# A first pass of attention that takes one head and all keys at a time

## The chip, the cores and the metric

The kernel runs on one core of a Trainium2 chip. The metric is the device time of one execution, in microseconds (us), as the median of the runs shown.

## The reference

One block of a gated cross-attention model, with batch 4, 1024 tokens, width 512, a context of width 1024, and 8 heads of 64. Cut to what matters:

```python
src_trans = einsum('bsf,of->bso', src, W_src) + b_src        # keys and values, from the context
tgt_trans = einsum('btf,of->bto', layernorm(x), W_tgt) + b_tgt   # queries
src_trans, tgt_trans = both times the mask
scores = einsum('bthd,bshd->bhts', q, k) / sqrt(64)
scores = where(src_mask == 0, -inf, scores)
attn = softmax(scores, axis=-1)
tgt_update = einsum('bhts,bshd->bthd', attn, v)
x = x + tanh(g_xattn) * (concat([layernorm(x), tgt_update]) @ W_out.T + b_out)
x = x + tanh(g_ffn) * ffn(layernorm(x))     # int8-like activations, ternary weights, depthwise conv of 3, silu
```

## The kernel before

The program has four stages, one after the other: queries and the part of the output that doesn't need attention (A), keys and values (B), attention (C), and the feed-forward part (D). Only stage C is changed. Each engine has its own hand-written program; semaphores order them.

**Two passes over the scores.** A pair of heads has its 64-row operands in partitions 0 to 63 (head 0) and 64 to 127 (head 1), so that two matmuls, one of each head, use separate halves of TensorE's rows. There are 16 pairs (4 batches x 4 pairs), numbered g. The *first pass* (`tops`, PE line 1244) computes rough scores, queries down the partitions, keys along the columns, only to find each query's maximum. VectorE (line 926) reads them from PSUM, adds the mask's row and keeps the minimum of the negated values. The *second pass* (`score`, line 1260) computes the scores exactly, keys down the partitions, 512 queries along the columns, in four terms (high x high, low x high, high x low, and the row maxima by a small matmul), and ScalarE exponentiates 1024 columns (both heads) at once (line 684). `product` (line 1272) multiplies the exponentials by the values, and each of its two matmuls appears as two passes in the trace.

**Units and macros.** Both passes are cut into 256 units, 16 per pair of heads. A unit of the first pass is 128 queries, both heads and 512 of the 1024 keys: two matmuls. A unit of the second pass is 128 keys, both heads and 512 queries: eight matmuls. TensorE's loop runs 134 *macros* s. A macro holds the second pass of units 2s and 2s+1, the products of units 2s-2 and 2s-1, and the first pass of units 2s+22 and 2s+23; the first pass is `LEAD` = 22 units ahead, and its first 22 units are a lead-in of their own before macro 0. From macro 117 on no first pass is left.

**PSUM banks.** Of the eight banks of 512 columns, the first pass uses bank 4 (head 0) and bank 5 (head 1), the second pass 0 and 1 (even units) and 2 and 3 (odd units), the products 6 and 7. Bank 4 also takes the transpose of the row maxima (`rows`, line 1279) and the row sums (`sums`, line 1285). Bank 5 also takes the output projection (`project`, twelve matmuls in `split_mm`, lines 1224 to 1226). VectorE counts what it has read from the two banks in the semaphores `dve_free4` and `dve_free5`. A first pass waits on the one and the other.

**What stands at a macro's end.** After the products of some macros come: `rows` in macros 8g-3; `sums` in macros 4k+6 for block k of 8 units; `project` in the 24 macros 32 to 39, 64 to 71 and 96 to 103, and eight more in the last macros. VectorE then casts the transposed maxima twice (lines 944 and 946), or transposes the sums (`zt`, line 950), or adds the projection to `bx` (line 975, `finish`). In the macro behind a `sums`, VectorE inverts the sums and normalises (`inverse`, `normal`); two macros behind it ScalarE copies the high part (`upper`, line 692) between its two exponentials and VectorE subtracts it (`lower`, line 968) between its reads for the two units of the first pass. GpSimd adds up the exponentials (line 667).

In macros with a projection the two banks of the first pass are taken in reverse order. VectorE collects 32 minima in `nmv` and folds the two key halves in one small reduction per pair of heads (line 933).

## Time and profile before

| what | value |
|---|---|
| runs before | 1923.99, 1928.58 and 1927.51 us; median 1927.51 |
| the profiled execution | 1929.86 us, of which the span of the trace is 1928.0 us |
| busy in the span | TensorE 1684.4 us (87%), VectorE 1216.9 (63%), ScalarE 780.3 (40%), GpSimd 729.0 (38%) |
| chain that ended last | TensorE 62%, issue 19%, GpSimd 7%, VectorE 6%, DMA 5% |
| its first lines | second pass (L1260) 13%, products (L1272) 12%, keys and values (L1224 to L1226) 9% each, first pass (L1244) 6% |
| VectorE's reads of the first pass (L926) | 512 of 689 ns, 333.4 us busy |

A row of a timeline gives the start in the span, the length, the engine, the line and the operation with output and inputs, how many instructions were merged, and in brackets the idle time before and what ended it. A matmul's length includes its way through the array, so that neighbours overlap; the distance between two starts is what one costs. PEld is the load of a matmul's weights. `64*128` and `128*64` are the part of the array that a matmul uses.

### The profile page before, as it was taken

The page shows a single profiled execution, that of the slowest core. Times are in us where ns is not written, and L with a number is a line of the kernel's source. Part 1 is how long each engine was busy: PE and PEld are TensorE (multiplying, and loading weights), DVE is VectorE, ACT ScalarE, POOL GpSimd, SP SyncE. Part 2 cuts the span into 40 slices and gives each one's busy share as a digit, 9 for nine tenths or more (in the row PEclk, how much of TensorE's full clock was granted, in tenths as well). Part 3 has the DMA queues.
Part 4 walks back from the last instruction along what each step waited for, and adds up shares of the span by engine and source line. Part 5 has one row for each costly group of instructions (what it writes and reads, how often), then busy time and mean ns, then how long its engine had stood idle before and what let it go on. Part 6 is the DMA issues. An engine that isn't in the chain of part 4 may idle for free.

```text
span 1928.0 us, 24398 instructions
## 1 busy us (share of the span) xinstructions
PE 1684.4 (87%) x8738; PEld 1038.8 (54%) x8738; DVE 1216.9 (63%) x2270; ACT 780.3 (40%) x793; POOL 729.0 (38%) x317
## 2 busy tenths in 40 slices
PE   6887899999997699999999999999856785967867
PEld 5666678888885344455445444544433443534434
DVE  6777645343433567755765676465269979799793
ACT  2111122222210044433442344245318766787676
POOL 1121000000000088866885688578606134062340
PEclk9989999999998599999999999999979798997988
DMA  6656547444444511114111412041130030120201
GB/s 233 229 181 206 179 170 243 154 149 152 171 145 152 180 56 56 56 66 143 56 57 66 143 57 100 12 143 35 44 131 1 1 131 0 38 92 0 88 1 44
DMA packets 104676, 200.59 MB, mean 104 GB/s; under 512 B 7568, under 2 KB 27024, under 8 KB 104592
## 3 DMA queue, kind: packets, MB, share of 16 engines
q1 hardware_dynamic: 104592, 199.49, 29.5%
q8 instruction: 50, 0.82, 0.2%
q14 instruction: 34, 0.28, 0.0%
HBM read 127.90 MB, written 71.57 MB: 103 GB/s over the span
## 4 chain that ended last, share of the span: by engine, by line
PE 62%; issue 19%; POOL 7%; DVE 6%; DMA 5%; SPq 1%; ACT 1%; POOLq 0%; DVEq 0%; ACTq 0%
PE ps L1260 13%; PE ps L1272 12%; PE ps L1224 9%; PE ps L1226 9%; PE ps L1225 9%; PE ps L1244 6%; DMA wraw<-in_w2T 5%; POOL h_first L672 4%; POOL h_third L672 2%; PE ps L1285 2%; DVE junk L926 1%; PE ps L1461 1%; DVE h_first L1179 1%; POOL acc L667 1%; DVE gp L1158 1%
## 5 line engine op out<-in xcount | busy, mean ns | idle before, releaser
L667 POOL TENSOR_TENSOR acc<-acc,pr 128x1024 f32<-128x1024 f32 x192 | 457.7, 2384 | 118.7 <-ACT pr L684 99.6
L684 ACT ACTIVATE pr<-ps,mcol 128x1024 f32<-128x1024 f32 x256 | 284.3, 1114 | 405.1 <-PE ps L1260 402.3
L926 DVE CUSTOM_DVE_ANT_0 junk<-ps,mbias 128x512 bf16<-128x512 f32 x512 | 333.4, 689 | 171.8 <-PE ps L1244 168.0
L1272 PE MATMUL ps<-pr,vv 128*64 128x512 f32 x1024 | 273.3, 616 | 0.0
L672 POOL TENSOR_TENSOR h_first<-h_first,last_tap 128x1024 f32<-128x1024 f32 x44 | 104.8, 2385 | 306.2 <-ACT last_tap L804 306.2
L650 POOL MEMSET nmt<- 128x128 f32 x1 | 0.2, 204 | 449.1 <-DMA w_ternary<-wtb 449.1
L1244 PE MATMUL ps<-kh,qh 64*128 64x512 f32 x512 | 136.8, 475 | 26.3 <-DVE nmv L926 17.6
L1244 PEld LDWEIGHTS ps<-kh,qh 64*128 64x128 f32 x512 | 57.5, 193 | 148.3 <-issue 101.7
L1419 PE MATMUL ps<-xiT,w1q 128*128 128x512 bf16 x512 | 125.1, 393 | 5.9 <-ACT xiT L790 5.9
L1461 PE MATMUL ps<-w2q,hq 128*128 128x512 bf16 x512 | 120.8, 390 | 2.5 <-ACT hq L840 1.8
L667 POOL TENSOR_TENSOR acc<-pr 128x1024 f32<-128x1024 f32 x32 | 76.8, 2399 | 110.8 <-ACT pr L684 110.8
L1260 PE MATMUL ps<-qh,kh 64*128 64x512 f32 x512 | 116.2, 445 | 0.0
L1448 PE MATMUL ps<-ident,h_first 128*128 128x128 f32 x352 | 57.8, 317 | 66.2 <-DVE h_first L1179 51.8
L1260 PE MATMUL ps<-qh,kl 64*128 64x512 f32 x512 | 102.5, 392 | 0.0
L1260 PE MATMUL ps<-maug,aug 64*128 64x512 f32 x512 | 102.3, 391 | 0.0
L1260 PE MATMUL ps<-ql,kh 64*128 64x512 f32 x512 | 102.0, 390 | 0.0
L1224 PE MATMUL ps<-chh,wsh 128*128 128x512 f32 x256 | 99.7, 389 | 1.7 <-DVE chl L1091 1.7
L1224 PE MATMUL ps<-wsh,chh 128*128 128x512 f32 x256 | 99.7, 389 | 0.3 <-DVE cst L1133 0.3
L1226 PE MATMUL ps<-wsh,chl 128*128 128x512 f32 x256 | 99.6, 389 | 0.0
L1225 PE MATMUL ps<-wsl,chh 128*128 128x512 f32 x256 | 99.6, 389 | 0.0
L1225 PE MATMUL ps<-chl,wsh 128*128 128x512 f32 x256 | 99.6, 389 | 0.0
L1226 PE MATMUL ps<-chh,wsl 128*128 128x512 f32 x256 | 99.6, 389 | 0.0
(152 smaller groups left out, 3179.7 us busy)
## 6 DMA issues: line engine op xcount, KB each, us to landing
craw<-in_ctxT SPq DMA_DIRECT2D x8, 2048.0 KB, 9.7
xa<-in_x SPq DMA_DIRECT2D x8, 1024.0 KB, 6.4
wraw<-in_w1T SPq DMA_DIRECT2D x16, 512.0 KB, 7.3
wraw<-in_w2T SPq DMA_DIRECT2D x16, 512.0 KB, 7.6
q_split<-kqh SPq DMA_DIRECT2D x32, 256.0 KB, 2.0
q_split<-kql SPq DMA_DIRECT2D x32, 256.0 KB, 2.3
base<-lna SPq DMA_DIRECT2D x8, 1024.0 KB, 9.1
k_split<-kqh SPq DMA_DIRECT2D x32, 256.0 KB, 2.2
```

The lines of the kernel that those rows point to most:

```text
L667: nc.gpsimd.tensor_tensor(acc[:, blk % 2, :], first, pr[:, (8 * blk + j) % NP, :], ALU.add).then_inc(pool_acc, 1)
L672: nc.gpsimd.tensor_tensor(h[j % 3], h[j % 3], last_tap[j % 2][:], ALU.add).then_inc(pool_tap, 1)
L684: act.activation(pr[:, u % NP, :], ps[:, 2 * (u % 2):2 * (u % 2) + 2, :].rearrange("p a t -> p (a t)"), ACT.Exp, bias=mcol[:, (u // 64) * ...
L926: dve.tensor_tensor_reduce(out=junk[:, e, :], in0=ps[:, 4 + e, :], in1=mbias[:, b % 2, kk * CH:(kk + 1) * CH], scale=-1.0, scalar=3.0e38, ...
L1224: pe.matmul(acc, lh, rh, start=k == 0, stop=False)
L1225: pe.matmul(acc, lh, rl, start=False, stop=False)
L1226: last = pe.matmul(acc, ll, rh, start=False, stop=k == n - 1)
L1244: last = pe.matmul(ps[:, 4 + e, :], qh[g % 3][64 * e:64 * e + 64, i * P:(i + 1) * P], kh[g % 3][64 * e:64 * e + 64, kk * CH:(kk + 1) * CH] ...
L1260: last = pe.matmul(ps[:, 2 * (u % 2) + e, :], of_keys[64 * e:64 * e + 64, :], of_tokens[64 * e:64 * e + 64, :], start=w == 0, stop=w == 3)
L1272: last = pe.matmul(ps[64 * e:64 * e + 64, 6 + blk % 2, :], vv[:, g % 2, j, 64 * e:64 * e + 64], pr[:, u % NP, e * CH:(e + 1) * CH], start= ...
L1419: last = pe.matmul(ps[:, 2 * (j % 2) + t, :], w1q[:, k, j * P:(j + 1) * P], xiT[:, k, t * 512:(t + 1) * 512], start=k == 0, stop=k == KD - 1)
L1461: last = pe.matmul(ps[:, i % 2, :], hq[:, i % 2, j, :], w2q[:, j, :], start=j == 0, stop=j == KH - 1)
```

## The change

The first pass is cut the other way: a unit is now 128 queries, *one* head and all 1024 keys, so that its two matmuls are the two key halves of one head, in banks 4 and 5. Even units are head 0, odd units head 1. One VectorE operation reads both banks, 1024 columns, and writes the minimum straight into `nmt`, which gets two halves used in turn; `nmv`, the fold and `dve_nm` go. Both banks now have one semaphore, `dve_free`, and a planner (`take`) notes for each use of the banks which use it has to wait for. In the lead-in odd units use banks 0 and 1.

TensorE's loop is written as two streams. In each of ten slots there is one matmul of head 0 and one of head 1. Head 0 has the even unit's first pass in slots 0 and 1 and its scores in slots 2 to 9; head 1 has its scores in slots 0 to 7 and the odd unit's first pass in slots 8 and 9. Then come the products of both units, with nothing between them, and `rows`, `sums` and `project` as before. The semaphore for ScalarE is now raised by head 0's last score, in slots 5 and 9.

```diff
+        def take(use, banks):
+            after[use] = max(held.get(bank, 0) for bank in banks)
+            done[use] = len(done) + 1
+            for bank in banks:
+                held[bank] = done[use]
+
+        def first_bank(n):
+            return 4 if n >= LEAD or n % 2 == 0 else 0
+
         for n in range(LEAD):
-            use4["a", n], use5["b", n] = len(use4), len(use5)
+            take(("m", n), (first_bank(n), first_bank(n) + 1))
...
         def c_dve(dve):
             def tops(n):
-                g, i, kk = n // 16, n % 16 // 2, n % 2
-                b = g // PAIRS
+                g, i, e = n // 16, n % 16 // 2, n % 2
+                b, bank = g // PAIRS, first_bank(n)
                 if n % 64 == 0 and b:
                     bias(b)
-                if n % 16 == 0 and g:
-                    dve.wait_ge(dve_nm, g)
-                for e, free, use in heads(n):
-                    dve.wait_ge(pe_mx, n + 1)
-                    c = (8 * e + i) * 2 + kk
-                    dve.tensor_tensor_reduce(out=junk[:, e, :], in0=ps[:, 4 + e, :], in1=mbias[:, b % 2, kk * CH:(kk + 1) * CH], scale=-1.0,
-                                             scalar=3.0e38, op0=ALU.add, op1=ALU.min, accum_out=nmv[:, c:c + 1]).then_inc(free, 1)
-                if n % 16 == 15:
-                    dve.wait_ge(dve_free4, use4["a", n] + 1)
-                    dve.wait_ge(dve_free5, use5["b", n] + 1)
-                    if g:
-                        dve.wait_ge(pe_mt, g)
-                    dve.tensor_reduce(nmt[:, 0:16], nmv[:].rearrange("p (c k) -> p c k", k=2), AX.X, ALU.min).then_inc(dve_nm, 1)
+                if n % 16 == 0 and g >= 2:
+                    dve.wait_ge(pe_mt, g - 1)
+                dve.wait_ge(pe_mx, n + 1)
+                if n:
+                    dve.wait_ge(dve_free, done["m", n - 1])
+                dve.tensor_tensor_reduce(out=junk[:], in0=ps[:, bank:bank + 2, :].rearrange("p a t -> p (a t)"), in1=mbias[:, b % 2, :], scale=-1.0,
+                                         scalar=3.0e38, op0=ALU.add, op1=ALU.min, accum_out=nmt[:, g % 2, 8 * e + i:8 * e + i + 1]).then_inc(dve_free, 1)
...
         def c_pe(pe):
-            def tops(n):
-                g, i, kk = n // 16, n % 16 // 2, n % 2
-                if n % 16 == 0:
+            def first(n, half):
+                g, i, e = n // 16, n % 16 // 2, n % 2
+                if n % 16 == 0 and half == 0:
                     pe.wait_ge(sp_qk[g % 3], 32 * (g // 3 + 1))
-                for e, free, use in heads(n):
-                    if use:
-                        pe.wait_ge(free, use)
-                    last = pe.matmul(ps[:, 4 + e, :], qh[g % 3][64 * e:64 * e + 64, i * P:(i + 1) * P],
-                                     kh[g % 3][64 * e:64 * e + 64, kk * CH:(kk + 1) * CH], start=True, stop=True)
-                last.then_inc(pe_mx, 1)
-
-            def score(u):
+                if half == 0 and after["m", n]:
+                    pe.wait_ge(dve_free, after["m", n])
+                scores = pe.matmul(ps[:, first_bank(n) + half, :], qh[g % 3][64 * e:64 * e + 64, i * P:(i + 1) * P],
+                                   kh[g % 3][64 * e:64 * e + 64, half * CH:(half + 1) * CH], start=True, stop=True)
+                if half:
+                    scores.then_inc(pe_mx, 1)
+
+            def score(u, w, e):
...
-                if u >= 2:
+                if w == 0 and u >= 2:
                     pe.wait_ge(act_p, u - 1)
+                if w == 0 and u < 2:
+                    pe.wait_ge(dve_free, done["m", LEAD - 1])
...
+                term = pe.matmul(ps[:, 2 * (u % 2) + e, :], of_keys, of_tokens, start=w == 0, stop=w == 3)
+                if w == 3 and e == 0:
+                    term.then_inc(pe_st, 1)
...
             for s in range(MACROS):
-                for a in range(2):
-                    if 2 * s + a < UNITS:
-                        score(2 * s + a)
-                    if a == 0 and 2 * s + LEAD < UNITS:
-                        tops(2 * s + LEAD)
-                for a in range(2):
-                    if 0 <= 2 * s - 2 + a < UNITS:
-                        product(2 * s - 2 + a)
-                    if a == 0 and 2 * s + LEAD + 1 < UNITS:
-                        tops(2 * s + LEAD + 1)
+                for slot in range(10):
+                    u, n = 2 * s + (slot - 2) // 4, 2 * s + LEAD
+                    if slot < 2 and n < UNITS:
+                        first(n, slot)
+                    if slot >= 2 and u < UNITS:
+                        score(u, (slot - 2) % 4, 0)
+                    u, n = 2 * s + slot // 4, 2 * s + LEAD + 1
+                    if slot < 8 and u < UNITS:
+                        score(u, slot % 4, 1)
+                    if slot >= 8 and n < UNITS:
+                        first(n, slot - 8)
+                for u in (2 * s - 2, 2 * s - 1):
+                    if 0 <= u < UNITS:
+                        product(u)
```

Two places where the order differs. On TensorE, the end of macro 10, which has the row sums, and the beginning of macro 11. Before (L1244 is the first pass, L1272 a product, L1285 the sums, L1260 the second pass):

```order
L1244 MATMUL ps<-kh_108,qh_107 128x512 [waits dve_free4]
L1244 MATMUL ps<-kh_108,qh_107 128x512 [waits dve_free5]
L1272 MATMUL ps<-pr,vv 64x512 [waits act_p]
L1272 MATMUL ps<-pr,vv 64x512
L1285 MATMUL ps<-acc,ones 64x512 [waits dve_free4,pool_acc]
L1285 MATMUL ps<-acc,ones 64x512
L1260 MATMUL ps<-qh_111,kh_112 128x512 [waits act_p]
L1260 MATMUL ps<-qh_111,kh_112 128x512
L1260 MATMUL ps<-qh_111,kl 128x512 x2
L1260 MATMUL ps<-ql,kh_112 128x512 x2
L1260 MATMUL ps<-maug,aug_101 128x512 x2
L1244 MATMUL ps<-kh_108,qh_107 128x512 [waits dve_free4]
```

And now (L1239 is the first pass, L1268 a product, L1280 the sums, L1256 the second pass):

```order
L1239 MATMUL ps<-kh_107,qh_106 128x512 [waits dve_free]
L1256 MATMUL ps<-maug,aug_101 128x512
L1239 MATMUL ps<-kh_107,qh_106 128x512
L1268 MATMUL ps<-pr,vv 64x512 [waits act_p]
L1268 MATMUL ps<-pr,vv 64x512
L1268 MATMUL ps<-pr,vv 64x512 [waits act_p]
L1268 MATMUL ps<-pr,vv 64x512
L1280 MATMUL ps<-acc,ones 64x512 [waits dve_free,pool_acc]
L1280 MATMUL ps<-acc,ones 64x512
L1239 MATMUL ps<-kh_107,qh_106 128x512 [waits dve_free]
L1256 MATMUL ps<-qh_110,kh_111 128x512 [waits act_p]
```

The first pass has moved out from between the products, in front of them and to the head of the next macro, directly behind the sums. On VectorE, macro 12, two macros behind those sums. Before (L926 reads a bank, the second L926 row of each is its accumulator, L963 normalises, L968 is the low part):

```order
L963 TENSOR_TENSOR un<-ps,rb 128x512 [waits pe_pv,dve_inv]
L926 ISA junk,nmv<-ps,mbias 128x512 [waits pe_mx]
L926 ISA nmv 128x1
L926 ISA junk,nmv<-ps,mbias 128x512 [waits pe_mx]
L926 ISA nmv 128x1
L968 TENSOR_TENSOR ul<-un,uh 128x512 [waits act_uh]
L926 ISA junk,nmv<-ps,mbias 128x512 [waits pe_mx]
```

And now (L928 reads both banks, L959 normalises, L964 is the low part):

```order
L959 TENSOR_TENSOR un<-ps,rb 128x512 [waits pe_pv,dve_inv]
L928 ISA junk,nmt<-ps,mbias 128x1024 [waits dve_free,pe_mx]
L928 ISA nmt 128x1
L964 TENSOR_TENSOR ul<-un,uh 128x512 [waits act_uh]
L928 ISA junk,nmt<-ps,mbias 128x1024 [waits dve_free,pe_mx]
```

The low part keeps its place between the two units' reads, and each unit has one read in place of two.

## Rows read from the trace of the kernel before

**Rows 1.** The windows by stage: lead-in, attention, feed-forward; engines' busy us, granted clock, DMA.
```profile
core 0: us, PE busy (x) PEld busy (x) DVE busy (x) ACT busy (x) POOL busy (x), PEclk, DMA share, GB/s
618.77:668.24 49.47, 29.40 (x45) 11.95 (x46) 29.09 (x89) 0.00 (x0) 0.00 (x0) 0.50 0.62 218
678.51:1376.05 697.54, 693.12 (x3921) 334.84 (x3919) 427.27 (x1149) 292.86 (x283) 524.22 (x221) 1.00 0.21 73
1412.00:1928.00 516.00, 367.35 (x2193) 210.90 (x2192) 426.65 (x503) 356.56 (x295) 155.75 (x64) 0.88 0.14 49
```

**Rows 2.** The timeline of TensorE, macro 42: start, length, line, operation, count.
```profile
902.80 0.50 PE L1260 MATMUL ps<-qh,kh 64*128 64x512 f32 x2
903.14 0.40 PE L1260 MATMUL ps<-qh,kl 64*128 64x512 f32 x2
...
903.83 0.39 PE L1244 MATMUL ps<-kh,qh 64*128 64x512 f32 x2
...
905.06 1.08 PE L1272 MATMUL ps<-pr,vv 128*64 128x512 f32 x4
906.07 0.49 PE L1244 MATMUL ps<-kh,qh 64*128 64x512 f32 x2
906.50 1.08 PE L1272 MATMUL ps<-pr,vv 128*64 128x512 f32 x4
907.46 1.08 PE L1285 MATMUL ps<-acc,ones 128*64 128x512 f32 x4
```

**Rows 3.** The timeline of TensorE in macro 120, where no first pass is left.
```profile
1339.42 1.94 PE L1272 MATMUL ps<-pr,vv 128*64 128x512 f32 x8
1341.29 0.50 PE L1260 MATMUL ps<-qh,kh 64*128 64x512 f32 x2
```

**Rows 4.** The timeline of VectorE in macros 42 and 44.
```profile
904.27 0.69 DVE L926 CUSTOM_DVE_ANT_0 junk<-ps,mbias 128x512 bf16<-128x512 f32 x1 [1.06 <-PE ps L1244]
...
904.88 0.69 DVE L926 CUSTOM_DVE_ANT_0 junk<-ps,mbias 128x512 bf16<-128x512 f32 x1
...
908.57 0.72 DVE L950 STREAM_TRANSPOSE zt<-ps 128x512 f32<-128x512 f32 x1 [0.65 <-PE ps L1285]
...
916.10 0.69 DVE L968 TENSOR_TENSOR ul<-un,uh 128x512 fp32r<-128x512 f32 x1
```

**Rows 5.** The timeline of the lead-in: VectorE's first read, later its reads and TensorE's weight load.
```profile
621.24 0.69 DVE L926 CUSTOM_DVE_ANT_0 junk<-ps,mbias 128x512 bf16<-128x512 f32 x1
...
630.63 0.69 DVE L926 CUSTOM_DVE_ANT_0 junk<-ps,mbias 128x512 bf16<-128x512 f32 x1
...
631.38 0.28 PEld L1244 LDWEIGHTS ps<-kh,qh 64*128 64x128 f32 x1 [0.33 <-DVE nmv L926]
632.21 0.69 DVE L926 CUSTOM_DVE_ANT_0 junk<-ps,mbias 128x512 bf16<-128x512 f32 x1 [0.88 <-PE ps L1244]
```

**Rows 6.** The timeline of TensorE and VectorE at macros with a projection.
```profile
848.69 1.08 PE L1285 MATMUL ps<-acc,ones 128*64 128x512 f32 x4 [0.49 <-DVE nmv L926]
...
1378.68 0.39 PE L1226 MATMUL ps<-wo2h,ul 128*128 128x512 f32 x1
...
1379.17 0.75 DVE L975 SCALAR_TENSOR_TENSOR bx<-ps,cst,bx 128x512 f32<-128x512 f32 x1 [4.14 <-PE ps L1226]
...
1380.07 0.47 PE L1224 MATMUL ps<-wo2h,uh 128*128 128x512 f32 x1 [1.01 <-DVE bx L975]
```

**Rows 7.** The timeline of ScalarE in macro 44.
```profile
914.44 1.12 ACT L684 ACTIVATE pr<-ps,mcol 128x1024 f32<-128x1024 f32 x1 [2.46 <-PE ps L1260]
915.45 0.62 ACT L692 ACTIVATE uh<-un 128x512 fp32r<-128x512 f32 x1
```

**Rows 8.** The timeline of TensorE and VectorE at a transpose of the row maxima.
```profile
777.49 0.33 PE L1279 MATMUL ps<-ident,nmt 128*128 128x128 f32 x1
777.75 0.50 PE L1260 MATMUL ps<-qh,kh 64*128 64x512 f32 x2
...
778.17 0.28 DVE L946 TENSOR_TENSOR mt<-ps,mt 16x128 fp32r<-16x128 f32 x1
```

More of the change, by code:

```diff
@@ L334, in flamingo_gated_block @@
         MACROS = 134
-        use4, use5, inv = {}, {}, {}
+        done, after, held, inv = {}, {}, {}, {}
+        def take(use, banks):
[5 more added lines that the diff above has]
+            return 4 if n >= LEAD or n % 2 == 0 else 0
         for n in range(LEAD):
-            use4["a", n], use5["b", n] = len(use4), len(use5)
+            take(("m", n), (first_bank(n), first_bank(n) + 1))
             if n == 15:
-                use4["t", 0] = len(use4)
+                take(("t", 0), (4,))
                 inv["row", 0] = 1
@@ L343, in flamingo_gated_block @@
                 if n < UNITS:
-                    use4["a", n], use5["b", n] = len(use4), len(use5)
+                    take(("m", n), (4, 5))
             if s - 1 in ZBLK:
@@ L1258, in score @@
-                for w, (of_keys, of_tokens) in enumerate(terms):
-                    for e in range(2):
-                        last = pe.matmul(ps[:, 2 * (u % 2) + e, :], of_keys[64 * e:64 * e + 64, :], of_tokens[64 * e:64 * e + 64, :],
-                                         start=w == 0, stop=w == 3)
-                last.then_inc(pe_st, 1)
+                if w == 0 and u < 2:
+                    pe.wait_ge(dve_free, done["m", LEAD - 1])
+                keys, tokens, rows = slice(j * P, (j + 1) * P), slice(t * CH, (t + 1) * CH), slice(64 * e, 64 * e + 64)
@@ L1276, in rows @@
             def rows(g):
-                pe.wait_ge(dve_nm, g + 1)
-                pe.wait_ge(dve_free4, use4["t", g])
-                pe.transpose(ps[:, 4, 0:P], nmt[:], ident[:]).then_inc(pe_mt, 1)
+                pe.wait_ge(dve_free, max(after["t", g], done["m", 16 * g + 15]))
+                pe.transpose(ps[:, 4, 0:P], nmt[:, g % 2, :], ident[:]).then_inc(pe_mt, 1)
             def sums(blk):
                 pe.wait_ge(pool_acc, 7 * (blk + 1))
-                pe.wait_ge(dve_free4, use4["z", blk])
+                pe.wait_ge(dve_free, after["z", blk])
                 for e in range(2):
@@ L1296, in c_pe @@
             pe.wait_ge(pool_zero, 4)
[L1297 to L1312 removed]
+            for n in range(LEAD):
+                first(n, 0)
+                first(n, 1)
+                if n == 15:
+                    rows(0)
+            for s in range(MACROS):
+                for slot in range(10):
[12 more added lines that the diff above has]
+                        product(u)
                 if s in TURNS:
```

47 lines of the change are left out of this document (17 added, 30 removed).

## The prediction

> **What bounds the kernel now.** I read the windows by stage first [rows 1]. The attention stage runs from 678.51 to 1376.05 us. TensorE is busy for 693.1 of those 697.5 us at a granted clock of 1.00, while VectorE has 427 us, ScalarE 293 and GpSimd 524. TensorE is the bound there and everything is priced as its time. In the lead-in ahead (618.77 to 668.24) it is the other way: TensorE and VectorE hand one pair of PSUM banks to and fro, and the clock is at 0.50. The feed-forward stage after 1412 isn't touched and is taken as it is.
>
> The timeline of one macro [rows 2] gives the prices. I write times from its first matmul, and call two matmuls side by side, one of each head, a slot. The first slot takes 0.34 (902.80 to 903.14), each further one 0.23 (three to 903.83), and the turn from the last slot to a product 0.31 (four slots after 903.83 end at 904.75; the product starts at 905.06). A product followed by anything in the other shape takes 1.01 (905.06 to 906.07), and a first pass between two products takes 0.43. So a plain macro is 906.50 + 1.01 - 902.80 = 4.71 us. At the end of the stage, where no first pass is left, two adjacent products take 1339.42 to 1341.29 = 1.87 us [rows 3], so 0.86 + 1.01.
>
> **The plain macro.** Now there are ten slots and then two products. Slot 9 would start at 0.34 + 8 x 0.23 = 2.18, the products at 2.49, and the next macro at 4.36: a gain of 0.35. But the first pass in slots 8 and 9 writes the banks that slots 0 and 1 filled, and waits until VectorE has read both. VectorE starts 0.44 after the slot that it needs (903.83 to 904.27 [rows 4]), so at 0.34 + 0.44 = 0.78. The trace of before has no read of 1024 columns. Two reads of 512 follow each other at 0.61 of which 0.08 is the accumulator's, so 512 more columns add 0.53, and 0.69 + 0.53 = 1.22 (bounds: 1.38 as two whole reads, 1.06 as columns alone). It ends at 2.00. TensorE's next weight load follows a VectorE read by 0.06 in the lead-in (630.63 + 0.69 = 631.32, load at 631.38 [rows 5]). So slot 8 begins at 2.06 in place of 1.95, and as its weights come late it takes 0.34: slot 9 at 2.40, products at 2.71 and 3.57, next macro at **4.58**. The change is -0.13 in each of the 117 macros that still carry a first pass: **-15.2 us**. (Without the slot-8 wait it would be -0.35; with a read of 1.38 about +0.03.) The second read has its data at 2.84, ends at 4.06, and so is done before 4.58.
>
> **The waits at slot 0.** Before, the first pass stood behind four slots of scores. Now it stands at the very front of a macro, and on TensorE's queue all ten slots are behind it. Whatever VectorE last does with banks 4 and 5 is therefore waited for in the open. Four cases:
>
> - *Row sums, every fourth macro.* The sum's matmuls start at 4.43, VectorE's transpose starts 1.11 later and takes 0.72 (907.46, 908.57 [rows 2, 4]). A restart after another shape follows by 0.15 (1379.17 + 0.75 to 1380.07 [rows 6]); I take 0.11 between this and 0.06. The next macro starts at 6.38, which is 1.80 more than a plain one, where it is 0.95 more today (907.46 + 1.01 - 902.80 = 5.67). That is +0.85. Of 28 such macros with a first pass behind, 22 have no projection that hides the transpose: **+18.7**.
> - *Two macros later.* VectorE's low part of the normalised rows stands between the two reads and waits for ScalarE's copy, which stands behind the exponential of the even unit. That unit now ends its scores in slot 5 (1.26) and not in slot 3. Exponential at 1.26 + 0.44 = 1.70, with VectorE's distance from a slot to its reader, copy 1.01 later and 0.62 long (914.44, 915.45 [rows 7]), so until 3.33; low part 3.37 to 4.06 (0.69, [rows 4]). The second read then runs 4.06 to 5.28, and the next macro starts at 5.39 in place of 4.58: +0.82 in 27 macros, **+22.1**. Today the same chain fits: the low part begins at 916.10 and nobody waits for it.
> - *Row maxima to rows.* The small transpose starts at 4.58, VectorE's two casts end 0.96 later (777.49 to 778.17 + 0.28) and the restart is 0.11; unstalled the step takes 0.26 (777.49 to 777.75 [rows 8]). +0.80 in the 11 macros where no projection follows: **+8.8**.
> - *Projection, 24 macros.* From the last of its twelve matmuls to the restart of TensorE behind VectorE's update takes 1378.68 to 1380.07 = 1.39 [rows 6], measured where the kernel already has this wait; the plain turn is 0.31. +1.08 each: **+25.9**. Against this, nine macros with a projection today stand still for 0.49 and restart late because the banks are read in turn (848.69 [rows 6]); now the read is over by 4.06, ahead of the sum at 4.43. About -0.6 each: **-5.4**.
>
> **Ends of the stage.** In macros 117 to 127 there is no first pass but the heads stay two slots apart, so ten slots hold eight slots' work: 11 x 2 x 0.23 = **+5.1**. In the lead-in two pairs of banks now alternate. Today a unit takes (668.24 - 621.24) / 22 = 2.14 us, of which VectorE reads 1.30 (0.61 + 0.69); it starts reading at 621.24 [rows 1, 5]. Behind a released bank pair the matmuls need 0.06, 0.83 to the first half's data (631.38 to 632.21) and 0.46 for the second half (a slot at half the clock), 1.35 in all, and then the read itself 1.22, for every two units. So a unit costs about 1.28: 2.5 to the first read + 22 x 1.28 + 2.5 for the row transpose, which nothing overlaps, = 33.2. **-16.3** (-13 if the second half's weights aren't loaded ahead). The small VectorE reduction per pair of heads, which folded the minima of the two key halves, goes, and so do half of the reads; both lie beside TensorE's work and are taken at nothing beyond what stands above; ScalarE and GpSimd have room (GpSimd 524 of 697 us, and the macros get longer).
>
> **Sum.** -15.2 + 18.7 + 22.1 + 8.8 + 25.9 - 5.4 + 5.1 - 16.3 = +43.7 us on the profiled run's 1929.9 us, so 1973.6. The median of the runs is 2.4 us lower: **1971 us**, 2.3% slower.
>
> **A rule on the weight loads.** In the lead-in the second head's weight load waits until its own bank has been read (631.38), and no later load passes it. The Trainium skill (TensorE: Matmul & The Clock Gate, Step-by-step: what each phase is for) says that TensorE may pull a weight load ahead of running matmuls when the row groups don't conflict, and keeps the matmuls in order. By that rule the restart's extra 0.11 would be hidden at each of some 84 waits, -9 us; the late slot in the row speaks against it.
>
> **Rivals.**
> *Faster: the waits are not in the open.* If a held first pass held only its own head, and the other head's matmuls ran on past it, the four slot-0 terms and the slot-8 wait would go: -41 - 5.4 + 5.1 - 16.3 = -58, so 1870 us. The waits are 75.5 + 117 x 0.22 = 101 us in all; this case decides once more than 44 of them, 43%, are hidden. For it: the two heads use separate rows of the array and separate banks. Against it: 848.69 and 1380.07 show the whole engine idle behind one waiting matmul. 7%.
> *Near no change:* the same, for about half of the waits. 6%.
> *Slower still: the clock.* In the lead-in TensorE is busy 29.4 of 49.5 us and is granted 0.50 [rows 1]. The new waits of 0.8 to 1.1 us come in 78 or so macros. If one in five of these let the clock fall for a macro, which would then cost about 4 us more (ten slots and two products at half the clock, 4.36 more at the most), that is +60: 2030 us. Against it: the stage as it is stays at 1.00 through the idles of 0.49 at 848.69; idles of 0.8 to 1.1 no row of it shows. The Trainium skill (TensorE: Matmul & The Clock Gate, A second HAM failure mode: psum-queue depth-cycling) tells of a kernel whose short idles between groups of matmuls, while PSUM banks are cycled, made the clock swing; this is the case that speaks against the change. 7%.
> *The heads don't run side by side* when their matmuls belong to different steps: ten slots at 0.43 or so, +2.0 x 117 = +234: 2205 us. Today's pairs already differ in weights, data and bank. 3%.
> The forecast keeps 77%.
>
> **Chances.** A measurement tells about 0.3% (6 us) from no change. Faster 0.08 (the first rival and a stray of the second), same 0.05, slower 0.87. For the range: no slot-8 wait takes 26 us off, 1945; a read of 1.30 with restarts of 0.15 everywhere adds some 20 us, 1992. I take 1943 to 1995, which leaves out the rivals on either side.
>
> **What the profile after would show.** Plain macros of 4.58 us (4.36 if slot 8 doesn't wait); products as groups of eight passes at 1.87; VectorE reads of 1.22; TensorE idle 0.8 to 1.1 us ahead of the first pass behind each sum, projection and row transpose and two macros after each sum; the lead-in some 33 us long. Wrong would be: macros behind a sum as short as plain ones, a granted clock under 1.00 in the stage, or slots of more than 0.23.

## The result, and the profile after

The changed kernel takes **1961.62 us** (median of 4 runs, 1960.06 to 1961.83) where the kernel before took 1926.83 in the same comparison (4 runs, 1923.99 to 1928.58): a ratio of 1.018, 95% interval 1.0163 to 1.0198, so 1.8% slower. The forecast was 1971 us, in a range of 1943 to 1995. The profiled execution took 1961.83 us, with a span of 1960.0.

The windows by stage of the changed kernel, with the columns of [rows 1]: the lead-in, attention from macro 2 to the last sum ahead of the final projections, and the rest.

```profile
core 0: us, PE busy (x) PEld busy (x) DVE busy (x) ACT busy (x) POOL busy (x), PEclk, DMA share, GB/s
614.56:649.88 35.32, 25.64 (x46) 10.51 (x47) 28.52 (x48) 0.00 (x0) 0.00 (x0) 0.50 0.83 290
659.69:1406.43 746.74, 679.84 (x3921) 365.23 (x3919) 404.63 (x672) 283.43 (x283) 524.08 (x221) 1.00 0.19 68
1406.43:1960.00 553.57, 394.30 (x2294) 229.82 (x2292) 436.78 (x516) 358.44 (x297) 161.62 (x67) 0.89 0.14 49
```

TensorE has *less* to do in the attention stage than before (679.8 us in place of 693.1, since products now stand together), but it stands idle for 67 us of it, where it stood idle for 4. The five waits listed below add up to those 67 us. The granted clock stayed at 1.00. The page puts 54% of the chain that ended last on TensorE (62% before) and 8% on VectorE (6%). Who was waited for, in the list of waits from 660 to 1420 us (columns: who waited, for whom, us in total, times, longest):

```profile
PE ps L1239 <- DVE bx L971: 20.8, 24, 0.9
PE ps L1239 <- DVE zt L946: 18.0, 22, 0.8
PE ps L1239 <- DVE nmt L928: 16.4, 24, 1.0
PE ps L1239 <- DVE mt L942: 7.5, 11, 0.7
PE ps L1220 <- DVE nmt L928: 4.1, 6, 0.7
```

These are the four slot-0 waits of the prediction: 24 behind projections, 22 behind sums, 11 behind row transposes, and those for a read. Of the 24 for a read, 21 are macros two behind a sum (0.59 to 0.69 us each), and three are at slot 8, where VectorE prepared the mask's row first (1.03 to 1.04 us); six more macros two behind a sum have a projection, which waits for the read instead (L1220). Now the timeline of TensorE around one of each (L1239 is the first pass, L1256 the second, L1268 the products, L1280 the sums):

```profile
900.10 0.50 PE L1239 MATMUL ps<-kh,qh 64*128 64x512 f32 x1
...
902.07 0.39 PE L1256 MATMUL ps<-ql,kh 64*128 64x512 f32 x1
902.16 0.49 PE L1239 MATMUL ps<-kh,qh 64*128 64x512 f32 x1
...
902.49 0.39 PE L1239 MATMUL ps<-kh,qh 64*128 64x512 f32 x1
902.82 1.94 PE L1268 MATMUL ps<-pr,vv 128*64 128x512 f32 x8
904.59 1.03 PE L1280 MATMUL ps<-acc,ones 128*64 128x512 f32 x4
906.43 0.49 PE L1239 MATMUL ps<-kh,qh 64*128 64x512 f32 x1 [0.82 <-DVE zt L946]
...
909.14 1.94 PE L1268 MATMUL ps<-pr,vv 128*64 128x512 f32 x8
911.01 0.50 PE L1239 MATMUL ps<-kh,qh 64*128 64x512 f32 x1
...
913.73 1.94 PE L1268 MATMUL ps<-pr,vv 128*64 128x512 f32 x8
916.36 0.46 PE L1239 MATMUL ps<-kh,qh 64*128 64x512 f32 x1 [0.69 <-DVE nmt L928]
```

The macro from 900.10 carries the sums: 6.33 us (5.67 in [rows 2]). The one from 906.43 is a plain macro: 911.01 - 906.43 = 4.58, and the next one, two behind the sums, takes 5.35. The products stand together (909.14 to 911.01 = 1.87, as in [rows 3]), and head 1's first pass at 902.16 is 0.09 late against head 0's slot beside it (902.07). VectorE in the same stretch:

```profile
900.87 1.22 DVE L928 CUSTOM_DVE_ANT_0 junk<-ps,mbias 128x1024 bf16<-128x1024 f32 x1 [1.30 <-PE ps L1239]
...
905.66 0.72 DVE L946 STREAM_TRANSPOSE zt<-ps 128x512 f32<-128x512 f32 x1 [1.50 <-PE ps L1280]
...
914.38 0.69 DVE L964 TENSOR_TENSOR ul<-un,uh 128x512 fp32r<-128x512 f32 x1 [1.36 <-ACT uh L694]
914.99 1.22 DVE L928 CUSTOM_DVE_ANT_0 junk<-ps,mbias 128x1024 bf16<-128x1024 f32 x1
```

The read of 1024 columns takes the 1.22 us of the forecast; 256 of them have a mean of 1222 ns. It begins 0.44 behind the slot that it needs (900.43 to 900.87) and ends at 902.09, and the first pass that wants its banks starts at 902.16. The low part has waited for ScalarE's copy until 914.38 and keeps the second read back until 914.99, so that the read ends at 916.21 and TensorE starts again at 916.36.

### The profile page after: what moved, and what is told of

It is laid out like the page before. It is cut to its first block, busy times and chain, and to the rows that moved or that the text cites. A ratio compares the mean times of both kernels' runs of the same rounds, so it can differ in the third digit from the quotient of the medians.

```text
span 1960.0 us, 24095 instructions
## 1 busy us (share of the span) xinstructions
PE 1664.0 (85%) x8738; PEld 1065.9 (54%) x8738; DVE 1194.5 (61%) x1742; ACT 770.7 (39%) x793; POOL 728.3 (37%) x317
## 4 chain that ended last, share of the span: by engine, by line
PE 54%; issue 21%; POOL 9%; DVE 8%; DMA 5%; ACT 1%; SPq 1%; POOLq 0%; ACTq 0%; DVEq 0%
PE ps L1256 9%; PE ps L1220 9%; PE ps L1268 9%; PE ps L1222 9%; PE ps L1221 9%; PE ps L1239 6%; POOL h_first L674 5%; DMA wraw<-in_w2T 4%; DVE junk L928 3%; POOL h_third L674 3%; PE ps L1460 2%; POOL acc L669 1%; PE ps L1280 1%; DVE bx L971 1%; ACT uh L694 1%
## 5 line engine op out<-in xcount | busy, mean ns | idle before, releaser
L928 DVE CUSTOM_DVE_ANT_0 junk<-ps,mbias 128x1024 bf16<-128x1024 f32 x256 | 313.0, 1222 | 155.5 <-PE ps L1239 152.5
L1239 PE MATMUL ps<-kh,qh 64*128 64x512 f32 x512 | 195.5, 467 | 79.6 <-DVE nmt L928 24.5
L1268 PE MATMUL ps<-pr,vv 128*64 128x512 f32 x1024 | 247.7, 605 | 0.0
L1256 PE MATMUL ps<-qh,kh 64*128 64x512 f32 x512 | 205.1, 420 | 0.7 <-DVE nmt L928 0.7
L1256 PE MATMUL ps<-maug,aug 64*128 64x512 f32 x512 | 191.9, 391 | 0.0
L1256 PE MATMUL ps<-qh,kl 64*128 64x512 f32 x512 | 191.6, 391 | 0.0
L1256 PE MATMUL ps<-ql,kh 64*128 64x512 f32 x512 | 191.1, 390 | 0.0
L1239 PEld LDWEIGHTS ps<-kh,qh 64*128 64x128 f32 x512 | 79.3, 195 | 192.7 <-DVE nmt L928 78.9
L1268 PEld LDWEIGHTS ps<-pr,vv 128*64 128x64 f32 x1024 | 62.2, 136 | 120.0 <-issue 119.7
L1220 PE MATMUL ps<-chh,wsh 128*128 128x512 f32 x256 | 99.7, 389 | 1.7 <-DVE chl L1087 1.7
L1256 PEld LDWEIGHTS ps<-qh,kh 64*128 64x128 f32 x512 | 90.7, 185 | 19.0 <-issue 6.0
L1220 PE MATMUL ps<-wsh,chh 128*128 128x512 f32 x256 | 99.7, 389 | 0.3 <-DVE cst L1129 0.3
```

The costliest lines, as they stand in the source:

```text
L928: dve.tensor_tensor_reduce(out=junk[:], in0=ps[:, bank:bank + 2, :].rearrange("p a t -> p (a t)"), in1=mbias[:, b % 2, :], scale=-1.0, sca ...
L1220: pe.matmul(acc, lh, rh, start=k == 0, stop=False)
L1239: scores = pe.matmul(ps[:, first_bank(n) + half, :], qh[g % 3][64 * e:64 * e + 64, i * P:(i + 1) * P], kh[g % 3][64 * e:64 * e + 64, half ...
L1256: term = pe.matmul(ps[:, 2 * (u % 2) + e, :], of_keys, of_tokens, start=w == 0, stop=w == 3)
L1268: last = pe.matmul(ps[64 * e:64 * e + 64, 6 + blk % 2, :], vv[:, g % 2, j, 64 * e:64 * e + 64], pr[:, u % NP, e * CH:(e + 1) * CH], start= ...
```

## The experiments

Each kernel is the changed kernel with one edit, unless it says otherwise. The comparisons had the kernel before at 1926.16 (e1 to e4), 1925.48 (e5, e7 to e9) and 1926.61 us (e6, e10).

My theory: the time is the occupancy of banks 4 and 5. A unit holds both of them from its first matmul to the end of the read, 0.34 + 0.44 + 1.22, and 0.06 until TensorE is back: 2.06 us, twice in a macro that wants to take 4.36. Nothing fits between, so each further user of these banks (sums, row maxima, projection) and each delay of a read (the low part) lengthens the macro. The rivals: the adjacent products or the two streams are themselves slow; the merged read is what costs; the waits are only partly in the open.

**e1_lower: the low part behind the second read.**

```diff
-                    if a == 0 and s - 2 in ZBLK:
+                    if a == 1 and s - 2 in ZBLK:
                         lower(ZBLK[s - 2])
```

> The changed kernel with one move: VectorE's low part of the normalised rows (lower) stands behind the second read of the macro, not between the two reads. If the forecast's second term is right (the low part waits for ScalarE's copy and holds up the second read, and that the next macro's first slot), the macros two behind a row sum fall from 5.24 to 5.34 us to the plain 4.58: 27 x 0.70 = -19 us, 1942 us. If something else set those macros (ScalarE's own delay, or a wait that only moves to another place), less than 5 us.

Measured: 1949.96 us (ratio to the kernel before 1.013, interval 1.0113 to 1.0147). That is 11.7 us less than the changed kernel and 8 us more than expected. The 28 macros two behind a sum fell by 18.4 us, close to the 19 expected (22 without a projection from 115.7 to 100.9 us, six with one from 55.5 to 51.9). But 6.9 us came back (the expectation of e6 puts it at up to 7.7): three macros in which the first unit of a new batch needs the mask's row took 7.74, 9.40 and 8.99 us in place of 6.86, and one with sums behind them 7.69 in place of 6.34. The timeline at the first of them, VectorE and GpSimd:

```profile
755.82 2.51 POOL L669 TENSOR_TENSOR acc<-pr 128x1024 f32<-128x1024 f32 x1 [1.17 <-ACT pr L686]
756.00 2.88 DVE L933 TENSOR_SCALAR mbias<-mbias 128x1024 f32<-128x1024 f32 x1
```

The operation that turns the mask into a bias takes 0.69 us at the stage's start. Here it began while GpSimd added, and took 2.88: until 758.88, 0.55 behind the end of the addition (758.33). In the changed kernel itself it began later in the addition, and took 2.23, again until 0.55 behind its end (757.85 + 2.38 = 760.23, and 760.78):

```profile
757.85 2.38 POOL L669 TENSOR_TENSOR acc<-pr 128x1024 f32<-128x1024 f32 x1 [1.19 <-ACT pr L686]
758.55 2.23 DVE L933 TENSOR_SCALAR mbias<-mbias 128x1024 f32<-128x1024 f32 x1
...
762.10 0.49 PE L1239 MATMUL ps<-kh,qh 64*128 64x512 f32 x1 [1.04 <-DVE nmt L928]
```

In every kernel here in which VectorE does it beside an addition of GpSimd, it ends 0.55 or 0.56 us behind that addition, whether it took 1.22, 1.9 or 2.9 us. So the mask operation doesn't run slowly beside GpSimd; it stands still until GpSimd is done. The Trainium skill (SBUF — State Buffer, SBUF: two separate sides) says so: the port pair that VectorE and GpSimd share is locked for a whole instruction by whichever came first, and the other is fully blocked, where VectorE's operation is of a kind that wants that pair. The trace agrees.

**e2_banks: sums and row maxima in bank 2, projection in bank 3.** These banks hold the odd unit's scores, and are free once ScalarE has exponentiated them; the odd unit's scores come only in the middle of the next macro.

```diff
+                if w == 0 and after.get(("s", u, e)):
+                    pe.wait_ge(dve_free, after["s", u, e])
...
-                pe.transpose(ps[:, 4, 0:P], nmt[:, g % 2, :], ident[:]).then_inc(pe_mt, 1)
+                if g:
+                    pe.wait_ge(act_p, 16 * g - 4)
+                pe.transpose(ps[:, 2 if g else 4, 0:P], nmt[:, g % 2, :], ident[:]).then_inc(pe_mt, 1)
...
+                pe.wait_ge(act_p, min(8 * blk + 14, UNITS))
...
-                    last = pe.matmul(ps[64 * e:64 * e + 64, 4, :], ones...
+                    last = pe.matmul(ps[64 * e:64 * e + 64, 2, :], ones...
...
+                pe.wait_ge(act_p, min(64 * (b + 1) + 2 * i + 2, UNITS))
-                split_mm(pe, ps[:, 5, :],...
+                split_mm(pe, ps[:, 3, :],...
```

> The changed kernel with the row sums and the transposed maxima in bank 2 and the projection in bank 3 (an odd unit's score banks, which TensorE needs again only from slot 4 on), so that the first pass in slot 0 waits for nothing but the last read. If the slot-0 waits are what makes the change slower: sums 6.33 to 5.44 (22 times), transposed maxima 5.66 to 4.85 (11), projection 8.44 to 7.52 (24): -19.6 - 8.9 - 22.1 = -51 us, 1911 us, and the two-behind macros stay at 5.3. If these macros are long because of VectorE's work itself, the time moves by less than 10 us.

Measured: 1907.39 us (0.9902, 0.9885 to 0.9918), so the changed kernel with other banks for these three is 1% *faster* than the kernel before. TensorE's timeline at a sum (L1242 is the first pass, L1288 the sums):

```profile
905.38 1.94 PE L1273 MATMUL ps<-pr,vv 128*64 128x512 f32 x8
907.15 1.03 PE L1288 MATMUL ps<-acc,ones 128*64 128x512 f32 x4
908.11 0.49 PE L1242 MATMUL ps<-kh,qh 64*128 64x512 f32 x1
```

The first pass follows the sums by 0.96 with no idle time. Macros with sums take 5.44 in place of 6.33, with row maxima 4.91 for 5.66, with a projection 7.53 for 8.44; those two behind a sum stay at 5.25, which this edit shouldn't touch, and plain ones at 4.58.

**e3_two_reads: the unit's two halves read and released one by one.**

```diff
-                dve.tensor_tensor_reduce(out=junk[:], in0=ps[:, bank:bank + 2, :]..., accum_out=nmt[...]).then_inc(dve_free, 1)
+                for half in range(2):
+                    dve.tensor_tensor_reduce(out=junk[:, half * CH:(half + 1) * CH], in0=ps[:, bank + half, :],
+                                             ..., accum_out=nmv[:, c:c + 1]).then_inc(dve_free, 1)
+                if n % 16 == 15:
+                    dve.tensor_reduce(nmt[:, g % 2, 0:16], nmv[:].rearrange("p (c k) -> p c k", k=2), AX.X, ALU.min).then_inc(dve_free, 1)
...
-                if half == 0 and after["m", n]:
-                    pe.wait_ge(dve_free, after["m", n])
+                if after["m" if half else "h", n]:
+                    pe.wait_ge(dve_free, after["m" if half else "h", n])
```

> The changed kernel, but each unit is read by two operations of 512 columns again, each with its own bank's release (and the small fold per pair of heads is back). If the merged read costs by holding both banks until its end, slot 8 no longer waits: plain macros 4.58 to 4.36, -26 us, and some 5 us more where slot 0 needs only one of the banks: 1930 us. If the number of VectorE instructions mattered, it would be slower than the changed kernel by up to 256 x 0.08 = 20 us.

Measured: 1931.05 us (1.0022, 1.001 to 1.0034), the total expected, though not by the terms expected. Two reads of 512 back to back take VectorE 1.23 us until its next operation starts (916.99 to 918.22 in its timeline), where the one read takes 1.14 (757.41 to 758.55 in that of the changed kernel), but the first bank is given back after 0.69 of them. The plain macros directly behind a sum took 4.38 us in place of 4.58. But 11 others, directly behind a macro that is two behind a sum, took 4.72 to 4.76: the low part still delays the second read, and slot 1 now waits for its second half (926.17, 0.61 behind slot 0 in place of 0.34). The rest came mainly where slot 0 now waits for bank 4 alone: macros two behind a sum take 4.80 us (5.26), and the 24 with a projection 201.8 in all (213.2). Those with sums take 6.12 (6.33).

**e4_products: the kernel *before*, with its odd first pass ahead of the two products.** This brings the products together without streams or a merged read.

```diff
+                if 2 * s + LEAD + 1 < UNITS:
+                    tops(2 * s + LEAD + 1)
                 for a in range(2):
                     if 0 <= 2 * s - 2 + a < UNITS:
                         product(2 * s - 2 + a)
-                    if a == 0 and 2 * s + LEAD + 1 < UNITS:
-                        tops(2 * s + LEAD + 1)
```

> The kernel before with one move: the odd unit's first pass stands ahead of the two products, which are then adjacent; units, reads and banks as before. If keeping the products together were enough, plain macros would go from 4.71 to 4.36, -41 us: 1886 us. If the banks' release rules (first pass at slot 4, second bank read until 2.83, and the next first pass wants it at 2.18), plain macros take about 5.1 us, +49 us: 1976 us.

Measured: 1968.53 us (1.0214, 1.0197 to 1.0231). TensorE:

```profile
949.48 0.50 PE L1260 MATMUL ps<-qh,kh 64*128 64x512 f32 x2
...
951.71 1.10 PE L1244 MATMUL ps<-kh,qh 64*128 64x512 f32 x2
952.74 1.94 PE L1272 MATMUL ps<-pr,vv 128*64 128x512 f32 x8
954.61 0.50 PE L1260 MATMUL ps<-qh,kh 64*128 64x512 f32 x2
```

A plain macro is 954.61 - 949.48 = 5.13. The two units of the first pass (950.52 and 951.71) are now so close together that the second waits for the reads of the first, one bank after the other, and the products are held behind it: 1.03 us from 951.71 to 952.74 in place of 0.31. The same mechanism, without any of the change's other parts. Products side by side are worth having only if the first pass doesn't pay for it.

**e5_one_lead: banks 4 and 5 alone in the lead-in** (`first_bank` returns 4).

> The changed kernel with the lead-in's odd units in banks 4 and 5 too, so that one pair of banks is handed to and fro. If the lead-in's gain (49.5 us to 35.3) comes from the second pair of banks, a unit takes 0.06 + 0.83 + 0.46 + 1.22 = 2.57 us, the lead-in about 61 us: +26 us on the changed kernel's 1961.6, 1988 us, longer than even the lead-in of the kernel before, because one long read holds both banks. If it comes from the fewer and longer VectorE reads, it stays within 5 us of 1962.

Measured: 1985.32 us (1.0314, 1.0295 to 1.0333). From the first first pass to macro 2 it took 684.46 - 615.88 = 68.6 us in place of 45.1, and the macros were the same. The second pair of banks is worth 23.5 us to a lead-in of one-head units.

**e6_banks_lower, e7_all, e10_masks: the cures together.** e6 is e2 and e1, with the read of 1024 columns kept; e7 adds the two reads of e3; e10 is e7 with the mask's row prepared on ScalarE (for a mask of zeros and ones), which is 41% busy:

```diff
+                b = s // 32 + 1
+                if s % 32 == 15 and b < B:
+                    act.wait_ge(sp_mrow[b % 2], 16 * (b // 2 + 1))
+                    act.activation(mbias[:, b % 2, :], mbias[:, b % 2, :], ACT.Copy, bias=MASKED, scale=-MASKED).then_inc(act_mbias, 1)
...
                 if n % 64 == 0 and b:
-                    bias(b)
+                    dve.wait_ge(act_mbias, b)
```

> The changed kernel with sums, row maxima and projection in banks 2 and 3 (as e2) and the low part behind the second read (as e1), but with the one read of 1024 columns kept. If the edits add up: e2's 1907.4, less 18.4 for the macros two behind the sums, plus up to 7.7 for the stretched operation on the mask's row that e1 showed: 1889 to 1897 us. Against e7 (1873.7) it then says what the two separate reads bring when all else is cured: plain macros 4.58 against 4.39, 117 of them, 22 us, so 1895. Should plain macros also fall towards 4.39 here, the separate reads were worth nothing and it comes to 1874.

> Three edits on the changed kernel together: sums, maxima and projection in banks 2 and 3, two reads of one bank each, and the low part behind the second read. If the waits on banks 4 and 5 are the whole loss, no macro waits and a plain one takes 4.36 us, and the time is 1907 (the banks alone) - 26 - 18 + some us where the mask row is prepared beside GpSimd = 1868 us, ratio to before 0.970. If TensorE then meets another bound (GpSimd's 7 x 2.49 = 17.4 us per four macros of 18.3 with a sum), 1880 or more.

> The kernel of e7 (sums, row maxima and projection in banks 2 and 3, two reads of 512, low part behind the second read), with one edit: the mask's row of batches 1 to 3 is turned into its bias by ScalarE, six macros before the first read that needs it, instead of by VectorE directly ahead of that read. In e7 the VectorE operation took 2.88 to 2.92 us at each of the three places, beginning while GpSimd added, and the macros there took 6.94, 6.92 and 8.46 us where others with row maxima took 4.62. If the stretched operation is what they wait for, all three fall to about 4.62: 8.5 us less, 1865 us. If the wait has another cause (the change of pair of heads, the loads), they stay near 7 us and the time stays at 1874.

Measured: e6 1899.43 us (0.986, 0.9844 to 0.9876), e7 **1873.68** (0.9729, 0.9716 to 0.9742), e10 **1865.58** (0.9683, 0.9669 to 0.9696). e6 is 2.4 us above its range. The mask operation is not the reason, as the range had up to 7.7 us for it: it takes 2.89 us at all three places, as in e1, and TensorE waits 5.6 us for it in all. The edits don't add up as the expectation had it: the 18.4 us of e1 hold 3.6 for the six macros with a projection, which e2 alone had already brought to 45.2 us (55.5 in the changed kernel); in e6 they take 46.1. Between e6 and e7 lie 25.7 us, some 3.4 of them in the lead-in, so giving the halves back one by one is worth something even when nothing else is in the way: plain macros 4.58 and 4.39, with sums 5.44 and 5.23. In e10 all eleven macros with row maxima and no projection take 4.62 to 4.66 us, the three with a new mask among them (6.94, 6.92 and 8.46 in e7): the stretched operation was all that they waited for. The attention stage in the windows of e10 (columns as above), and in its timeline a whole plain macro (L1261 is the first pass, L1279 the second, L1291 the products):

```profile
659.17:1305.24 646.07, 645.57 (x3889) 358.51 (x3888) 409.70 (x1139) 283.49 (x283) 521.29 (x219) 1.00 0.22 78
```

```profile
704.93 0.50 PE L1261 MATMUL ps<-kh,qh 64*128 64x512 f32 x1
...
706.89 0.39 PE L1261 MATMUL ps<-kh,qh 64*128 64x512 f32 x1
706.90 0.39 PE L1279 MATMUL ps<-ql,kh 64*128 64x512 f32 x1
...
707.46 1.94 PE L1291 MATMUL ps<-pr,vv 128*64 128x512 f32 x8
709.32 0.50 PE L1261 MATMUL ps<-kh,qh 64*128 64x512 f32 x1
```

Attention now ends with TensorE busy for 645.6 of 646.1 us. Slot 8 starts beside its neighbour (706.89 and 706.90), and the macro takes 709.32 - 704.93 = 4.39, where the prediction had 4.36 without a wait.

**e9_pairs: e7 with the unit of the kernel *before*.** Both heads and 512 keys, behind the first and the last slot of the scores.

```diff
+                for k in range(8):
+                    for e in range(2):
+                        if 2 * s + k // 4 < UNITS:
+                            score(2 * s + k // 4, k % 4, 1 - e)
+                    if k in (0, 7) and 2 * s + LEAD + (k == 7) < UNITS:
+                        for e in range(2):
+                            first(2 * s + LEAD + (k == 7), e)
```

> As the run with all three edits, but a unit is again both heads and 512 keys, and the first pass stands behind the first and the last slot of the scores, both heads together; the products stay together. If the gain is the adjacent products and free banks, and neither the one-head unit nor the two shifted streams, it takes the same 1868 us within 0.3%. If the one-head unit is worth something of its own, it is slower by over 0.3% (6 us).

Measured: 1878.72 us (0.9764, 0.9751 to 0.9777), 5.0 us or 0.27% above e7, with plain macros of 4.43 in place of 4.39. About 2.1 of the 5.0 us are the mask operation once more, which the three macros with a new mask met at another moment (8.70, 8.64 and 7.09 us, for 6.94, 6.92 and 8.46). So the one-head unit by itself is worth a quarter of a per cent at the most; what gains in the macros is the adjacent products, and banks that are free when the first pass comes. The lead-in gains too: from the first first pass to macro 2 it takes 41.7 us here, where the kernel before takes 59.7. That is 18 of the 47 us between the two, and comes with the second pair of banks (e5). No run gave the kernel before that second pair alone.

**e8_fours: how far may one head's matmuls stand ahead in the queue?** The same twenty matmuls of a macro, but queued as four of head 1, four of head 0, and so on.

```diff
+                for k in (0, 4, 8):
+                    for step in heads[1][k:k + 4] + heads[0][k:k + 4]:
+                        step()
```

> The changed kernel with the same matmuls and waits, but TensorE's queue gets them four of one head, then four of the other (4 + 4, 4 + 4, 2 + 2), and not by turns. If a matmul can't start before its predecessor in the queue has (the strict order in which the two heads overlap only with their neighbours), ten slots become fifteen: +1.15 us in 117 macros, 2095 us. If each head's half of the array takes its own matmuls as they come, as the ends of the stage suggest (eight slots where I forecast ten), it stays within 10 us of 1962.

Measured: 1982.0 us (1.0293, 1.0277 to 1.0308), between the two times of the expectation and 20 us above the changed kernel. In the tail, where nothing is waited for, a macro takes 4.03 us, nearly the 3.92 of the changed kernel, and the heads run side by side:

```profile
1382.83 0.51 PE L1256 MATMUL ps<-qh,kh 64*128 64x512 f32 x2
1383.16 0.40 PE L1256 MATMUL ps<-qh,kl 64*128 64x512 f32 x2
1383.39 0.40 PE L1256 MATMUL ps<-ql,kh 64*128 64x512 f32 x2
```

Each row is two matmuls of like operands, one of each head. The second head's `qh,kh` stands behind four of the first head in the queue, and yet both are in the row at 1382.83, before the first head's next matmul at 1383.16. So it started ahead of three that stood before it. So matmuls on separate halves of the rows need not start in the order of the queue. Where head 0's group begins with a first pass that waits for a semaphore, it is otherwise:

```profile
937.12 0.49 PE L1256 MATMUL ps<-qh,kh 64*128 64x512 f32 x1
...
937.92 0.39 PE L1256 MATMUL ps<-maug,aug 64*128 64x512 f32 x1
938.01 0.50 PE L1239 MATMUL ps<-kh,qh 64*128 64x512 f32 x1
938.15 0.39 PE L1256 MATMUL ps<-qh,kh 64*128 64x512 f32 x1
```

Head 1's four run alone, and the waiting instruction starts only at 938.01, 0.05 us behind the end of VectorE's transpose of the sums (937.96), which it waits for. Head 1's next matmul stands behind it and starts at 938.15. Whether it is the wait alone that ends the freedom I didn't separate; plain macros took 5.05 to 5.5 us. The Trainium skill (TensorE: Matmul & The Clock Gate, Part 3: Packing small matmuls, The mechanism) states that matmuls start and end strictly in program order. The rows of this kernel differ, and they decide here.

## Why the prediction was right, and where its terms were off

The forecast term by term, on the profiled executions (macros from one start to the next):

| step | forecast | measured |
|---|---|---|
| plain macro | 4.71 to 4.58 | 4.58 |
| macro with sums | 6.38 | 6.33, 22 of them |
| two macros behind sums | 5.39 | 5.24 to 5.35 |
| macro with row maxima | 5.64 | 5.66, but the first 5.70 and three of 6.86 |
| 24 macros with a projection | +22 us in all | +17 us (196.0 to 213.2) |
| macros 117 to 127 | +5.1 us | 0 |
| lead-in | -16.3 us | -14.1 us (35.3 for 49.5) |
| read of 1024 columns | 1.22 | 1.22 |
| from the first first pass to the last projections | +43.7 us | +36.0 us |

(+22 is the prediction's 25.9 - 5.4, less 0.13 in each of the 24, plus 0.82 in the six that are also two behind a sum.) The stages ahead ended 4.2 us earlier in the profiled run of the changed kernel, 614.56 for 618.77; across the kernels here that moment lies between 614.1 and 618.8, with the same code ahead of it. With it +36.0 becomes the +32.0 us between the two profiled executions (1929.86 and 1961.83). The feed-forward stage kept its length. The forecast for the profiled execution, 1973.6, was 11.8 us above the measured one. Of these 4.2 lie ahead of the change, and the rest is what was left of misses both ways: some 13 us forecast too much (tail, projection, low part, sums) and some 7 too little (lead-in, mask's row, the stage's end). So the mechanism and its main terms were right, but that the total came this near is in part luck.

**Right:** what decided was that the first pass now stands at the head of a macro, and whatever VectorE does last with banks 4 and 5 is waited for in the open. The waits are there at their places, in number and nearly in size (0.82 us of idle TensorE behind sums, 0.69 behind row transposes, 0.59 to 0.69 for the delayed read and 0.84 to 0.94 behind projections, where the prediction names 0.8 to 1.1), e2 takes away three of the four, e1 the fourth, and the time turns from 1.8% slower to 1.4% faster (e6). The plain macro came out at 4.58, slot by slot, and e7 and e10 showed its 4.39 without the wait. The clock didn't fall, although TensorE now stood idle in 87 places for 0.6 to 1.0 us: it was granted 1.00 over the whole stage, and that rival did not come about.

**Wrong: "the heads stay two slots apart, so ten slots hold eight slots' work."** I took the tail's order from the queue. But the tail macros took 3.91 us as before, and the heads ran side by side:

```profile
1367.73 0.50 PE L1256 MATMUL ps<-qh,kh 64*128 64x512 f32 x2
...
1369.77 1.94 PE L1268 MATMUL ps<-pr,vv 128*64 128x512 f32 x8
```

Head 0's first matmul stands behind two of head 1 here and starts with the first of them; from 1367.73 to the products are 2.04 us, eight slots, not ten. e8 shows it over four. This also bears on the first rival, "the other head's matmuls ran on past it": matmuls do pass each other, but at none of the waits read here did one pass a matmul that waited for a semaphore; at 906.43 and 916.36 both heads start together behind the wait. By these rows the rival failed for that reason, and not because the queue is strict.

**Mis-sized:**

- *The lead-in's period.* A unit costs 1.38 us, not 1.28. The prediction had TensorE's chain of release, two matmuls and read set the period for two units. In the trace VectorE sets it, and has a gap between its reads:

```profile
618.57 1.23 DVE L928 CUSTOM_DVE_ANT_0 junk<-ps,mbias 128x1024 bf16<-128x1024 f32 x1
...
619.86 1.22 PE L1239 MATMUL ps<-kh,qh 64*128 64x512 f32 x2 [0.16 <-DVE nmt L928]
619.95 1.23 DVE L928 CUSTOM_DVE_ANT_0 junk<-ps,mbias 128x1024 bf16<-128x1024 f32 x1
```

  VectorE's reads are 1.38 apart where one takes 1.23. By the code each read waits for the semaphore of VectorE's own read before it, which the sum left out; with two reads, each waiting for the last but one, they follow without a gap (630.12, 630.73, 631.34 in e7), and the way from the first first pass to macro 2 took 41.6 us (e7) and with the one 44.9 (e6), 0.15 per unit. 22 x 0.10 are the 2.2 us.
- *The restart behind a projection* took 0.84 us of idle TensorE, and a plain macro with a projection went from 7.67 to 8.44, +0.77 where the sum had +0.95. The 1.39 from [rows 6] was measured between two projections; why a first pass starts 0.18 sooner than a projection does I didn't separate. In all 24 macros that is the 5 us in the table, as much as the tail.
- *The restart behind sums and reads* was put at 0.11. It took 0.05 behind the transpose of the sums (906.38 to 906.43), so that these macros are 6.33 and not 6.38, and 0.15 behind a delayed read (916.21 to 916.36).
- *The low part.* 5.24 to 5.35 in place of 5.39, -2 us in the 21 macros without a projection: the chain of exponential, copy and low part was right in each link (912.71, 913.73, 914.38), and 0.1 us shorter in its sum.
- *The mask's row.* Not in the sum at all, +3.6 us in three macros. The trace of before had the same operation at 1.2 to 1.6 us in place of 0.69, beside a slack that hid most of it (two of the three macros took 0.3 us longer than the others with row maxima). Looking up that one operation's durations would have shown it.
- *The stage's end.* Not in the sum either: from the start of the last macro to its first projection took 7.07 us in place of 5.62, +1.4, for the low part that the last section shows.

The range held; its lower end was set by a missing slot-8 wait, which e7 shows would have been worth 0.19 us in a macro, or 22 us, and not the 26 assumed in the prediction.

## What to carry to other kernels

Add up, for each PSUM bank, how long a unit holds it from its first matmul to the restart behind the reader, and compare it with the period of the loop: a merged read saves instructions but holds every bank until its end, and here it cost 26 us (e6 and e7) against two reads that released bank by bank. An edit that puts a waiting instruction where all later work of the engine stands behind it needs all rare users of the same banks moved out first. With that done, the halves released one by one and the mask's row moved, this one went from 1.8% slower to 3.2% faster; some 19 of the 61 us between the last kernel and the one before the change lie in the lead-in, with its second pair of banks. Adjacent work of one kind is worth only what the change of order doesn't take from the release of buffers (e4).

## What the hardware did that I had not expected

- Matmuls of the two 64-row halves started out of the queue's order: one that stood behind four of the other half started with the first of them, ahead of three (e8, 4.03 us a macro against 3.92), but none in the rows read started ahead of one that waited for a semaphore (938.01).
- VectorE's mask operation, from SBUF to SBUF, of 0.69 us, took 2.88 us when it began 0.18 us behind the start of a 2.5 us addition on GpSimd, and 2.23 when it began 0.70 behind; both ended 0.55 us behind the addition, as in all other kernels here. The same job on ScalarE took 1.06 us and nobody waited (e10).
- The low part subtracts one SBUF tensor from another. It took 0.69 us 28 times in the stage of the changed kernel: ScalarE's copy released it in a pause of GpSimd each time (at 914.38 GpSimd paused from 914.22 to 915.43). At the stage's end the two fell together, and here too VectorE ended 0.55 us behind GpSimd's addition (1407.28):

```profile
1402.41 7.67 POOL L669 TENSOR_TENSOR acc<-acc,pr 128x1024 f32<-128x1024 f32 x3
1404.94 2.89 DVE L964 TENSOR_TENSOR ul<-un,uh 128x512 fp32r<-128x512 f32 x1 [1.54 <-ACT uh L694]
...
1407.88 0.50 PE L1220 MATMUL ps<-wo2h,uh 128*128 128x512 f32 x1 [1.38 <-DVE ul L964]
```

  and TensorE stood idle for 1.38 us. Such a wait comes and goes with the phase of the two engines.
